# Forty dispatches ahead of the expert block instead of forty-eight, one Newton chain for two kinds of row scalars, and gathers that look three back instead of two

## What is computed

```python
x = x + 0.5 * ffn(layernorm(x))
x = x + attn(layernorm(x))
x = x + 0.5 * ffn(layernorm(x))

def ffn(x, wg, w1, b1, w2, b2):          # E = 8 experts, K = 2, capacity 1024
    scores = softmax(x @ wg)
    topv, topi = top_k(scores, 2); topv /= sum(topv)
    # position of a token at its expert: all first choices in token order,
    # then all second choices; positions of 1024 and more are dropped
    pos = position(topi); valid = pos < 1024
    h = relu(disp[topi, pos] @ w1 + b1);  y = h @ w2 + b2
    return sum_k (topv * valid)[k] * y[topi[k], pos[k]]

def attn(x):                             # linear attention, 16 heads of 8, per batch row
    q, k = elu(q) + 1, elu(k) + 1
    return (q @ (k^T v)) / (q . sum(k)) @ Wo.T + bo
```

## Time and profile before

| | us |
|---|---|
| median of 3 runs | 469.66 (466.82 to 471.26) |
| the profiled execution | 470.35 |
| its span, first to last instruction | 468.6 |
| blocks 1 and 2 | 0 to 170 |
| block 3, the attention | 170 to 321.3 |
| warm-up and block 4 up to the last expert's rows | 321.3 to 424 |
| last scatters, sums and stores | 424 to 468.6 |

### The profile page before, as it was taken

The page is one execution under the profiler, slowest core; times in us unless marked ns, Lnnn a source line. Parts: engine busy times, 40 slices in busy tenths (PEclk is TensorE's granted clock), DMA queues, the critical chain, the costliest instruction groups (busy, mean ns, idle before and its releaser), DMA issues. The chain is left out here.

```text
span 468.6 us, 6111 instructions
## 1 busy us (share of the span) xinstructions
PE 354.7 (76%) x1736; PEld 291.2 (62%) x1736; DVE 353.8 (75%) x1083; ACT 236.3 (50%) x431; POOL 273.4 (58%) x303
## 2 busy tenths in 40 slices
PE   6932769999999924686986889705799999999300
PEld 6912548888888713575775768605588888888200
DVE  6889178998888755578898885750579999999474
ACT  3688147666676604436355651420466776666100
POOL 9000577666664356665566766777756677766720
PEclk9999999999999976779777775555899999999855
DMA  8940314666666341111111111112512223311489
GB/s 235 358 149 1 96 46 142 203 206 195 210 229 214 118 130 45 45 45 41 39 45 44 54 52 50 57 52 87 179 63 75 88 90 92 96 40 41 161 323 300
DMA packets 47264, 55.48 MB, mean 118 GB/s; under 512 B 6694, under 2 KB 32832, under 8 KB 47232
## 3 DMA queue, kind: packets, MB, share of 16 engines
q1 hardware_dynamic: 34352, 35.40, 22.7%
q0 software_dynamic: 8512, 17.60, 13.0%
q10 hardware_dynamic: 4368, 2.10, 1.5%
HBM read 25.98 MB, written 29.10 MB: 118 GB/s over the span
## 5 line engine op out<-in xcount | busy, mean ns | idle before, releaser
L1121 ACT ACTIVATE hf<-psum,bcol 128x512 f32<-128x512 f32 x128 | 88.3, 690 | 64.3 <-PE psum L1056 61.2
L1025 POOL DMA_INDIRECT xg<-xn_dram,gidx x64 | 67.7, 1057 | 67.4 <-POOLq L1691 37.7
L1158 DVE TENSOR_TENSOR hl<-hf,hh 128x512 fp32r<-128x512 f32 x128 | 87.9, 697 | 5.4 <-ACT hh L1123 2.4
L1011 POOL DMA_INDIRECT yt_dram<-yg,target x64 | 70.4, 1100 | 33.4 <-DVE yg L1176 17.5
L1269 POOL DMA_INDIRECT yg<-y_dram,slot x64 | 61.3, 958 | 47.4 <-DMA yg<-y_dram,slot 30.5
L839 POOL DMA_INDIRECT xs_dram<-xns,place x64 | 62.3, 973 | 26.1 <-DMA xs_dram<-xns,place 15.0
L1052 PE MATMUL psum<-xh,wres 128*128 128x512 f32 x128 | 53.4, 417 | 3.4 <-ACT xh L1106 3.4
L1067 PE MATMUL psum<-hh,wres 128*128 128x512 f32 x128 | 53.0, 414 | 0.0
L1056 PE MATMUL psum<-xl,wres 128*128 128x512 f32 x128 | 51.0, 399 | 1.0 <-DVE xl L1147 1.0
L1069 PE MATMUL psum<-hh,wres 128*128 128x512 f32 x128 | 50.5, 395 | 0.0
L1068 PE MATMUL psum<-hl,wres 128*128 128x512 f32 x128 | 50.2, 393 | 0.0
(11 more groups left out here) (245 smaller groups left out, 732.9 us busy)
## 6 DMA issues: line engine op xcount, KB each, us to landing
yt_dram<-zeros SPq DMA_DIRECT2D x24, 256.0 KB, 3.5
xns<-yt_dram SPq DMA_DIRECT2D x24, 256.0 KB, 5.0
xs_dram<-zeros SPq DMA_DIRECT2D x16, 288.0 KB, 2.7
xg<-xs_dram SPq DMA_DIRECT2D x16, 288.0 KB, 2.8
wexp_raw<-in_L_ffn_w SPq DMA_DIRECT2D x16, 256.0 KB, 6.2
y_dram<-y_rows_out SPq DMA_DIRECT2D x16, 256.0 KB, 2.3
x_sb<-in_L_attn_x SPq DMA_DIRECT2D x8, 256.0 KB, 4.0
xn_dram<-xns SPq DMA_DIRECT2D x8, 256.0 KB, 5.9
```

Of the source, the lines that this page charges most:

```text
L1011: gp.indirect_dma_start(out=yt_dram, out_offset=bass.IndirectOffsetOnAxis(ap=target[:, j:j + 1], axis=0), in_=self.y_sb[:, s % YG, t], in_ ...
L1025: gp.indirect_dma_start(out=self.xg[:, s % 4, t], out_offset=None, in_=xn_dram, in_offset=bass.IndirectOffsetOnAxis(ap=gidx[:, j:j + 1], a ...
L1121: one = nc.scalar.activation(self.hf[:, c], bank[1 + c][:], ACT.Relu, bias=bcol[:, at:at + 1])
L1158: dve.tensor_tensor(self.hl[:, s % 2, c], self.hf[:, c], self.hh[:, s % 2, c].bitcast(F32), ALU.subtract).then_inc(hl_ready[c], 1)
```

## The change

Four edits, all in block 3 and at its border with block 4.

1. Part 2 is split. `dispatch_early` sends 40 dispatches: parts 0 and 1, and the first four tiles of part 2 (choice 1, then choice 0). `dispatch_late` sends the other four tiles of part 2 and then part 3, 24 dispatches, in block 4. `WIDE` still begins at d = 40.
2. `need_i` now has three levels: 40 landed dispatches where an expert has 256 first and 256 second choices among the first 20 tiles, 48 where only the old test holds, 64 else. PE gets one small matmul more for the early totals, and `needs` three more instructions on 8 values of one partition. PE's warm-up waits for dispatch 35 instead of 43, since its wait is written with `EARLY_SENT`.
3. In rounds 4 and 6 the 20 instructions of `row_scalar_steps` go. `scale_steps` takes 8 more `bn_aggr` first and runs its Newton chain 12 wide instead of 4. At its end one more instruction writes `rstd` and one more `nmr`. Parts 2 and 3 keep `row_scalar_steps`.
4. Gathers wait for gather i - 3 instead of i - 2.

```diff
-EARLY_SENT = 6 * (NT // 4)
+EARLY_SENT = 5 * (NT // 4)
+MORE_SENT = 6 * (NT // 4)
...
             def needs(self, dve, ch):
-                totals = self.choice_totals()
+                totals, early = self.choice_totals(), self.early_totals()
                 dve.wait_ge(counts_done, 5)
...
+                ch.then(dve.scalar_tensor_tensor(more[:], early[0:1, 0], float(EDGE), need[:], ALU.is_lt, ALU.max))
+                ch.then(dve.scalar_tensor_tensor(more[:], early[0:1, 1], float(EDGE), more[:], ALU.is_lt, ALU.max))
+                ch.then(dve.scalar_tensor_tensor(need[:], need[:], (K * NT - MORE_SENT) / (MORE_SENT - EARLY_SENT), more[:], ALU.mult, ALU.add))
-                dve.tensor_scalar(need_i[:], need[:], 16.0 * (K * NT - EARLY_SENT) / 4, 16.0 * EARLY_SENT / 4, ALU.mult, ALU.add).then_inc(needs_known, 1)
+                dve.tensor_scalar(need_i[:], need[:], 16.0 * (MORE_SENT - EARLY_SENT) / 4, 16.0 * EARLY_SENT / 4, ALU.mult, ALU.add).then_inc(needs_known, 1)
...
                 if part == 3:
+                    nc.tensor.matmul(self.early_totals(), ones_bf[:], self.before[:, 2, :, :, GT], start=True, stop=True)
...
-            def send(self, gp, place, part, k):
+            def send(self, gp, first, part, k, half=None):
                 gp.wait_ge(row_marked, 2 * part + 2)
-                for t in range(PT * part, PT * part + PT):
+                tiles = range(PT * part, PT * part + PT) if half is None else range(PT * part + GT * half, PT * part + GT * half + GT)
+                for t in tiles:
...
-                    d = PT * place + t - PT * part
-                    older = d - (NARROW if place < WIDE_FROM else WIDE)
+                    d = first + t - tiles[0]
+                    older = d - (NARROW if d < WIDE_FROM * PT else WIDE)
...
-                for part in range(3):
+                for part in range(2):
                     gp.wait_ge(placed, part + 1)
-                    self.send(gp, 2 * part, part, 1)
-                    self.send(gp, 2 * part + 1, part, 0)
+                    self.send(gp, 2 * PT * part, part, 1)
+                    self.send(gp, 2 * PT * part + PT, part, 0)
+                gp.wait_ge(placed, 3)
+                self.send(gp, 4 * PT, 2, 1, 0)
+                self.send(gp, 4 * PT + GT, 2, 0, 0)
             def dispatch_late(self, gp):
+                self.send(gp, 5 * PT, 2, 1, 1)
+                self.send(gp, 5 * PT + GT, 2, 0, 1)
                 gp.wait_ge(placed, 4)
-                self.send(gp, 6, 3, 0)
-                self.send(gp, 7, 3, 1)
+                self.send(gp, 6 * PT, 3, 0)
+                self.send(gp, 7 * PT, 3, 1)
...
-                        if i >= NARROW:
-                            gp.wait_ge(yg_in[(i - NARROW) % GT], landings(i - NARROW))
+                        if i >= WIDE:
+                            gp.wait_ge(yg_in[(i - WIDE) % GT], landings(i - WIDE))
...
                 def scale_steps(n):
                     u = n % 2
-                    v, y, a = (self.nwa[:, u, q] for q in range(3))
+                    part = {4: 0, 6: 1}.get(n)
+                    m = GT if part is None else GT + PT
+                    v, y, a = (self.nwa[:, u, q, 0:m] for q in range(3))
+                    if part is not None:
+                        ch.wait()
+                        for t in range(PT):
+                            ch.add(dve.bn_aggr(self.agg[:, u, GT + t], stats[:, PT * part + t]))
...
-                        to = self.rsa[:, u, 0] if square == 4.0 else y
-                        ch.add(dve.scalar_tensor_tensor(to, a, -3.0, y, ALU.add, ALU.mult))
-                        done = ch.n
+                        if square == 4.0:
+                            ch.add(dve.scalar_tensor_tensor(self.rsa[:, u, 0], a[:, 0:GT], -3.0, y[:, 0:GT], ALU.add, ALU.mult))
+                            done = ch.n
+                            if part is not None:
+                                ts = slice(PT * part, PT * part + PT)
+                                ch.add(dve.scalar_tensor_tensor(rstd[:, ts], a[:, GT:m], -3.0, y[:, GT:m], ALU.add, ALU.mult))
+                        else:
+                            ch.add(dve.scalar_tensor_tensor(y, a, -3.0, y, ALU.add, ALU.mult))
+                            done = ch.n
...
+                    if part is not None:
+                        ch.wait()
+                        dve.scalar_tensor_tensor(nmr[:, ts], self.agg[:, u, GT:m, 0], -1.0, rstd[:, ts], ALU.mult, ALU.mult).then_inc(rstd_done, 1)
...
-                others_at = {4: row_scalar_steps(ch, dve, 0, PT), 5: route.top2_steps(dve, ch, 0),
-                             6: row_scalar_steps(ch, dve, PT, 2 * PT), 7: route.top2_steps(dve, ch, 1)}
+                others_at = {5: route.top2_steps(dve, ch, 0), 7: route.top2_steps(dve, ch, 1)}
```

More of the change, by code:

```diff
@@ L193, in macaron @@
         need = sb("need", [1, E])
+        more = sb("more", [1, E])
         need_i = sb("need_i", [1, E], I32)
@@ L717, in choice_totals, with early_totals @@
                 return psum[:, 5, 256 + C + HEADS:256 + C + HEADS + 2 * K * E].rearrange("p (k e u) -> p k e u", e=E, u=2)
+            @staticmethod
+            def early_totals():
+                at = 256 + C + HEADS + 2 * K * E
+                return psum[:, 5, at:at + K * E].rearrange("p (k e) -> p k e", e=E)
             def needs(self, dve, ch):
-                totals = self.choice_totals()
+                totals, early = self.choice_totals(), self.early_totals()
                 dve.wait_ge(counts_done, 5)
@@ L1303, in __init__ @@
                 self.sta = new("sta", [P, 2, GT, 6])
-                self.agg = new("agg", [P, 2, GT, 2])
-                self.nwa = new("nwa", [P, 2, 3, GT])
+                self.agg = new("agg", [P, 2, GT + PT, 2])
+                self.nwa = new("nwa", [P, 2, 3, GT + PT])
                 self.rsa = new("rsa", [P, 2, 2, GT])
@@ L1512, in scale_steps @@
                     ch.wait(done)
-                    ch.add(dve.tensor_scalar(v, self.agg[:, u, :, 1], EPS, None, ALU.add))
+                    ch.add(dve.tensor_scalar(v, self.agg[:, u, 0:m, 1], EPS, None, ALU.add))
                     done = ch.n
@@ L1530, in scale_steps @@
                         ch.wait(done)
-                        to = self.rsa[:, u, 0] if square == 4.0 else y
-                        ch.add(dve.scalar_tensor_tensor(to, a, -3.0, y, ALU.add, ALU.mult))
-                        done = ch.n
+                        if square == 4.0:
[7 more added lines that the diff above has]
+                            done = ch.n
                         yield
                     ch.wait(done)
-                    dve.scalar_tensor_tensor(self.rsa[:, u, 1], self.agg[:, u, :, 0], -1.0, self.rsa[:, u, 0], ALU.mult, ALU.mult).then_inc(an_scale, 1)
+                    dve.scalar_tensor_tensor(self.rsa[:, u, 1], self.agg[:, u, 0:GT, 0], -1.0, self.rsa[:, u, 0], ALU.mult, ALU.mult).then_inc(an_scale, 1)
+                    if part is not None:
+                        ch.wait()
+                        dve.scalar_tensor_tensor(nmr[:, ts], self.agg[:, u, GT:m, 0], -1.0, rstd[:, ts], ALU.mult, ALU.mult).then_inc(rstd_done, 1)
                     yield
```

## The result

The changed kernel takes **451.92 us** (median of 5 runs, 450.76 to 456.17), against 469.66 for the kernel before in 5 runs on the same chip. The ratio is 0.9636 with a 95% interval of 0.9592 to 0.9681, so it is faster by 3.2 to 4.1%. On another chip the same kernel came to 0.9659 (0.9616 to 0.9702). The profiled execution took 456.2 us, the longest of the five, with a span of 454.4 us. It had lost 2.3 us before the attention began, in stages that the change does not touch.

What follows compares the result with a forecast made beforehand. The attention's block was taken to end on GpSimd, with VectorE nearly level, and the experts to run on TensorE. Border 9.0 plus gathers 5.2 less Newton 0.8 made 13.3 us off 469.66: 456.4 us, range 451.5 to 462.

Steps and rivals of the forecast that it cites:

- the 453 to 459.5: Case that both parts, the earlier border and VectorE's earlier part 1 marks, pay as summed; chance 0.63.
- The border, 9.0 us: Between attention and experts: with 40 dispatches ahead, the block's border moves from 321.34 to 312.3 us, 9.0 us earlier.
- The cover of the first load: At the experts' start: first rows arrive at 317.5 us, TensorE is ready at 320.4, so covered by 2.9 us.
- The gathers' pace: GpSimd's gathers in the attention: with three in flight they start 1.27 us apart instead of 1.53.
- The gathers' worth, 5.2 us: VectorE's waits on gathered rows in the attention's rounds shrink, bringing its part 1 marks 5.2 us earlier.
- More can't be had: Limit on the gathers' gain of 5.2 us: the waits that go were the only ones on gathers behind group 2.
- The Newton chain, a loss of 0.8 us: Rounds 4 and 6 on VectorE: one chain loses 0.8 us together, within bounds of 2.4 gain and 1.6 loss.
- the prediction's shorter chain: Round 4 on VectorE, from `k_sum` to the added rows: 2.3 us needed without the 20 instructions, instead of 4.4.
- The warm-up, kept at 8.1 us up to the turn: TensorE from the border to the first expert rows turned: 8.1 us as before, give or take 1.5 us.
- the stretch behind it: From TensorE's first turn of expert rows to the end: 139 us, unchanged.
- What is late next: Behind the 24 late dispatches, GpSimd's scatters come 4 to 5 us late, made up over 12 blocks at no cost.
- The rival of the full Newton gain: Rounds 4 and 6: the chain edit gains 2.4 us instead of losing, giving 453.1 us; chance 0.12.

Runs made afterwards that it cites:

- the one without the border: The changed kernel with 48 dispatches ahead of the border to block 4 again, as in the kernel before: 462.66 us, ratio 0.9876.
- the gathers alone: The kernel before with only its gathers changed, to wait for the one three back: 461.52 us, ratio 0.9815.
- border and gathers: The changed kernel with the two old Newton chains in rounds 4 and 6: 456.28 us, ratio 0.9714.
- border alone: The kernel before with only 40 dispatches ahead of the border and three levels in `need_i`: 463.35 us, ratio 0.9823.
- Newton alone: The kernel before with only the change to one Newton chain in rounds 4 and 6: 469.2 us, ratio 0.9978.
- shorter warm-up: The changed kernel with 20 instead of 50 warm-up transposes on TensorE: 453.53 us, ratio 0.9644.
- early test failing: The changed kernel with the early-count test made to fail for every expert, so the first load waits for 48 landed dispatches: 464.47 us, ratio 0.9883.
- filled pause: The changed kernel with 28 unused transposes in TensorE's wait ahead of round 6's first transposes: 450.56 us, ratio 0.9617.

## Why the prediction was right, and where it was off

The forecast was 456.4 us with a range of 451.5 to 462.0. 451.92 lies 0.4 us inside its lower end, and outside the 453 to 459.5 to which the forecast itself gave 0.63. The gain was 17.7 us where 13.3 were forecast. The two main mechanisms, the border and VectorE's waits on gathered rows, are right, but that the time still falls into the range owes something to chance. Its own steps:

1. **The border, 9.0 us: right in the traces.** With like rounds it measured 9.1 us (the changed kernel against the one without the border). In the times, where the pair was measured on one chip, it is 2.2% with the one chain and 1.0% without it, so its worth in the median is known only to some 5 to 10 us. The cover of the first load was sized at 2.9 us and measured 1 to 2; it held.
2. **The gathers' pace: right.** 1.26 us apart, as the dispatches from 40 on had shown. VectorE's waits on rows fell to 7.6 us where about 6 were expected.
3. **The gathers' worth, 5.2 us: right in the traces, too low in the times.** Up to the end of round 3 the prediction had 4.4 us and the changed kernel gained 4.2. With the gathers alone dispatch 16 came 5.0 us sooner, with border and gathers 6.4. The times of the gathers alone give 6.4 to 11.0 us, and what they give beyond the trace stays open. "More can't be had" counted only the waits on rows. It left out what the gathers do to TensorE's clock. In the ten profiles with the new gathers round 4 has a clock of 0.95 to 1.00 in eight and 0.72 and 0.75 in two; in the four with the old ones it has 0.72 to 0.86.
4. **The Newton chain, a loss of 0.8 us: wrong in sign.** The step that failed is the choice of the clock: I took the key sums at 2.09 us because the one row I had stood at the lower clock, and kept the full clock as a bound. The rounds of eight profiles side by side:

   | kernel | chains | round 4: clock, us | round 6: clock, us |
   |---|---|---|---|
   | before | two | 0.74, 13.17 | 0.60, 12.74 |
   | border alone | two | 0.72, 12.37 | 0.62, 12.64 |
   | border and gathers | two | 1.00, 12.31 | 0.62, 12.62 |
   | Newton alone | one | 0.73, 12.46 | 0.75, 11.65 |
   | shorter warm-up | one | 0.72, 12.18 | 0.62, 13.13 |
   | changed | one | 1.00, 10.33 | 0.61, 13.13 |
   | early test failing | one | 1.00, 10.32 | 0.73, 12.47 |
   | filled pause | one | 1.00, 10.33 | 1.00, 10.32 |

   With two chains the clock makes no difference in round 4: VectorE is busy for 11.6 us in it, and the round takes 12.3 to 12.4 us at either clock (in the kernel before, 0.9 us of waiting for rows is added). With one chain VectorE is busy for 9.9 us. The round can then be as short as 10.3 us, and whether it is depends on TensorE. At the full clock the chain takes 2.0 us off round 4. From `k_sum` to the added rows it took 2.2 us (222.68 to 224.91), which is the 2.3 of the prediction's shorter chain. At a clock of 0.72 the same round takes 12.18 us. In round 6, at 0.61, the chain costs 0.4 to 0.5, where the prediction had a loss of up to 0.8. The eight `bn_aggr` cost 0.63 us, priced at 0.7:

```profile
219.26 0.63 DVE L1530 BATCH_NORM_AGGREGATE agg<-stats 128x2 f32<-128x6 f32 x8
```

   Dispatch 16 came 7.0 us earlier where 4.4 were forecast, and nearly all of the difference is in round 4. So the gathers and the chain depend on each other: the new gathers make the full clock likelier, and the full clock makes the chain pay. The times neither show nor exclude this. The three ratios alone (0.9823, 0.9815, 0.9978) multiply to 0.962 beside the 0.9636 and 0.9659 of the whole, and gathers and chain without the border (0.9876) are no faster than the gathers alone (0.9815), on another chip.
5. **The warm-up, kept at 8.1 us up to the turn, took 7.1; the stretch behind it 138.7 instead of 139.1.** That is 1.5 us more. Against it stand 0.9 us by which dispatches 16 to 39 took longer (32.9 against 32.0). Over all runs with 50 transposes the warm-up lasted 7.0 to 8.5 us without regard to the idle time before it (8.22 behind 7.79 us, 6.97 behind 4.74, 8.28 behind 12.77), so this term is chance and was within the 1.5 us allowed for.
6. **What is late next: right.** The dispatches ended at 342.2. The first scatter began 26.8 us behind the first turn instead of 19.9, so it was 6.8 us late where 4 to 5 were forecast, and the loads for the sums moved with the experts. Dispatches 40 to 63 took 31.3 us (30.6 before), and four of the 24 were longer than usual, up to 1.49 us. Over all profiles, two to six of the 24 are longer than 1.05 us with 40 dispatches ahead of the border and none to three with 48, but the 24 together take 30.2 to 32.6 us with 40 and 30.6 to 32.1 with 48. A price of running more of them under the experts' casts is not to be seen in the whole. The rule of the Trainium skill's page SBUF — State Buffer (section on the two separate sides) points to such a price; that these longer ones are its lock is not shown here.

The gain that was missed is 4.4 us: 2.6 in the rounds, 1.5 less 0.9 in step 5, and the remaining 1.2 lie between the profiled executions and the medians. The rival of the full Newton gain, 453.1, was nearest to the result, and it got a chance of 0.12. Its mechanism held in round 4 alone: round 6 stayed at 0.61 and lost.

What stays open is why the clock holds in rounds 4 and 5 in one execution and not in another of the same program (0.72 with the short warm-up, whose rounds are the changed kernel's). The filled pause shows that activity of TensorE can hold it: in both kernels with it round 6 had a clock of 1.00, in the twelve profiles without it 0.60 to 0.75. I don't know what decides in a given execution.

## What to carry over

- What an edit on one engine pays can depend on the clock of another. The one chain saved VectorE 2.0 us in round 4 where TensorE ran at the full clock, and next to nothing at 0.72. Price each TensorE step of a loop at both clocks, and ask which of the two the new loop will have.
- A saving on one engine reaches the end only if the one level with it is moved too. The Newton chain gave nothing at dispatch 16 while GpSimd's gathers held it (107.5 and 107.9 us from round 0, 107.8 before).
- Before a transfer is allowed to wait for fewer rows, count what the data really puts there. The early test was right by counts that the inputs give, and its failing would have cost 7.6 us in the trace and 12 in the median.
- One profile is one execution. The same rounds ran at clocks of 0.72 and 1.00, and one edit measured 1.0% and 2.2% in two pairs of kernels. A term of 1 or 2 us is read from like stretches of several traces, not from the time.

## What the runs showed of the hardware

- Indirect DMAs of 128 rows issued back to back by GpSimd start 1.25 to 1.28 us apart; with the wait on the one two back it was 1.4 to 1.53. Waits on landed gathers fell from 30.5 us (44 of 64) to 1.5 us (5 of 64) when the wait went to the one three back.
- GpSimd's queue passes the border of a block before the last DMA ahead of it has been worked off: in the kernel before, TensorE is let go at 321.34 and the last dispatch of the block starts at 322.58; in the changed kernel both stand at 308.6.
- 28 transposes of no use in a pause of 4.65 us raised the granted clock of a round from 0.61 to 1.00 and shortened it from 13.1 to 10.3 us.
- The expert stage had a granted clock of 0.78, 0.90 and 1.00 in the same 12 us stretch of three profiles (border alone, before, changed); from the first turn to the end of the span it took 141.4, 139.1 and 138.7 us.
